# Triangle layers in one kernel: the variance of each chunk as four 32-column products, roots taken on 128 partitions and moved by small DMAs

## What is computed

```python
xn = layernorm(x, norm_g, norm_b)            # (x - mu) * rsqrt(var + eps) * g + b
left = xn @ Wl.T * m * sigmoid(xn @ Wlg.T)   # m: mask, layers 0 and 1 only
right = xn @ Wr.T * m * sigmoid(xn @ Wrg.T)
out_gate = sigmoid(xn @ Wog.T)
out = einsum('bikd,bjkd->bijd', left, right) # in layer 3: bimc,bmjc->bijc
out = layernorm(out, ...) * out_gate
return out @ Wout.T
```

## Time and profile before

| | |
|---|---|
| median of three runs | 2096.42 us |
| the profiled execution: its own time | 2098.47 us |
| its span | 2096.6 us |
| mean granted clock of TensorE | 0.958 of full speed |
| TensorE busy | 1779.0 us, 85% |
| ScalarE busy | 1372.8 us, 65% |
| VectorE busy | 1326.5 us, 63% |
| GpSimd busy | 1006.1 us, 48% |
| transfers | 496 MB, 237 GB/s in the mean |

### The profile page before, as it was taken

One profiled execution on the slowest core, in us unless ns is written; L12 is line 12 of the kernel. 1 busy time (PEld: TensorE's weight loads), 2 busy tenths in 40 slices (PEclk: granted clock), 3 DMA queues, 4 the chain that ended last, 5 costly groups with the idle time before them and its releaser, 6 DMA issues. The chain is left out here.

```text
span 2096.6 us, 40996 instructions
## 1 busy us (share of the span) xinstructions
PE 1779.0 (85%) x10389; PEld 1041.3 (50%) x10389; DVE 1326.5 (63%) x2984; ACT 1372.8 (65%) x2541; POOL 1006.1 (48%) x916
## 2 busy tenths in 40 slices
PE   0899997797998899995599799789799999699776
PEld 0445454685554445453255477633344444588433
DVE  7566666124763677776977388466377778344675
ACT  0577876355996788874499666477577787344554
POOL 0267678003991577776699300089222223000599
PEclk9999999798999999998899899999899999899999
DMA  7357876774996355546399666089547777845599
GB/s 325 123 181 235 246 231 218 268 290 170 366 367 232 101 188 173 187 149 253 135 349 366 242 217 209 32 316 375 193 150 232 234 236 216 296 179 222 187 397 377
DMA packets 326949, 496.17 MB, mean 237 GB/s; under 512 B 22828, under 2 KB 188463, under 8 KB 320439
## 3 DMA queue, kind: packets, MB, share of 16 engines
q1 hardware_dynamic: 326838, 494.93, 68.4%
HBM read 285.12 MB, written 197.13 MB: 230 GB/s over the span
## 5 line engine op out<-in xcount | busy, mean ns | idle before, releaser
L804 POOL TENSOR_TENSOR lo<-xn,hi 128x512 f16<-128x512 f32 x192 | 224.0, 1167 | 374.1 <-DVE hi L736 230.6
L601 PE MATMUL ps<-w_heads,hi 64*128 64x256 f16 x3072 | 294.0, 274 | 10.2 <-DVE sig L750 4.5
L1112 ACT ACTIVATE O<-ps 128x512 f32 (+1 forms) x144 | 151.8, 1054 | 190.5 <-PE ps L1033 190.5
L750 DVE SCALAR_TENSOR_TENSOR sig<-ps,largest,sig 128x512 f32<-128x512 f32 x256 | 180.8, 746 | 142.8 <-ACT sig L664 141.9
L664 ACT ACTIVATE sig<-ps,largest 128x512 f32<-128x512 f32 x384 | 246.2, 692 | 30.7 <-PE ps L601 28.6
L645 ACT ACTIVATE zs<-ps,shift 128x512 f32<-128x512 f32 x192 | 131.9, 687 | 191.4 <-PE ps L569 188.5
L1349 POOL TENSOR_TENSOR shared<-O,out_rs 128x128 f32<-128x128 f32 (+1 forms) x112 | 76.4, 684 | 370.8 <-DVE out_rs L1249 369.8
L601 PEld LDWEIGHTS ps<-w_heads,hi 64*128 64x128 f16 x3072 | 153.9, 95 | 167.1 <-DVE sig L750 67.3
L1397 PEld LDWEIGHTS ps<-ident,shared 128*128 128x128 f32 (+1 forms) x1024 | 120.0, 133 | 225.5 <-issue 96.4
L1397 PE MATMUL ps<-ident,shared 128*128 128x128 f32 (+1 forms) x1024 | 160.8, 282 | 75.6 <-POOL shared L1349 48.9
L601 PE MATMUL ps<-w_heads,lo 64*128 64x256 f16 x1536 | 213.5, 273 | 0.0
(11 more groups left out here) (164 smaller groups left out, 3724.3 us busy)
## 6 DMA issues: line engine op xcount, KB each, us to landing
shared<-left_right SPq DMA_DIRECT2D x34, 2048.0 KB, 12.0
shared<-gate SPq DMA_DIRECT2D x224, 256.0 KB, 4.6
gate<-gates SPq DMA_DIRECT2D x96, 512.0 KB, 2.9
x_dram<-shared SPq DMA_DIRECT2D x192, 256.0 KB, 4.3
shared<-x_dram SPq DMA_DIRECT2D x192, 256.0 KB, 4.7
xs<-x_dram SPq DMA_DIRECT2D x64, 512.0 KB, 4.2
left_right<-stage SPq DMA_DIRECT2D x64, 448.0 KB, 6.0
left_right<-shared SPq DMA_DIRECT2D x64, 448.0 KB, 5.7
```

The lines of the kernel that those rows point to most:

```text
L601: last = pe.matmul(PAIR[row][:, g, kb * S:kb * S + S], tokens[half, q % 8, at:at + P], k["w_heads"][half, part, :], start=(step == 0), sto ...
L750: dve.scalar_tensor_tensor(dst, pair(row, 1), k["largest"][:, 1:2], factor, ALU.mult, ALU.mult).then_inc(pair_read.sem, 1)
L804: pool.tensor_tensor(lo[:, q % 8, :], xn[:, q % 2, :], hi[:, q % 8, :], ALU.subtract).then_inc(c["lo_done"].sem, 1)
L1112: act.activation(o_of(ch), ps[h % 4 // 2][:, h % 2, :].rearrange("p (b g i) -> p b g i", b=2, g=2), ACT.Copy).then_inc(c["o_copied"].sem, 1)
```

## The change

The weights of `variance` have 32 columns instead of 128, and each chunk's product is made as four, one for each quarter of 128 tokens, into partitions 0, 32, 64 and 96 of the bank. The bank then holds 128 x 128 numbers, of which 16 rows in each 32 are the variances of a batch. Ln and Exp, and the split into three terms, work on 128 x 128. The terms go into a new tile, terms, and twelve DMAs from SP (three terms times four quarters, each 16 partitions of 256 bytes) move them into r_terms, where the spread reads them as before. A spread waits for the twelve moves of its batch. The split is cut in two halves, five and four steps ahead; the moves are issued three steps ahead. `variance` stands before the heads on TensorE, `root` before the sigmoids on ScalarE. CENTER is 14 and VARIANCE 13, so that 14 chunks are centered before the loop; x is loaded 18 ahead, into the same eight slots. hi and lo have four slots and not eight. SP's loop over the bodies is written out.

```diff
+QUAD = 32
...
-            "basis": sb("basis", [P, P]), "var_w": sb("var_w", [P, 2 * BATCH - 2 + P]), "ident": sb("ident", [P, P]),
+            "basis": sb("basis", [P, P]), "var_w": sb("var_w", [P, 2 * BATCH - 2 + QUAD]), "ident": sb("ident", [P, P]),
...
-                        ("xc_in", 4), ("gc_in", 4), ("x_out", 4)):
+                        ("xc_in", 4), ("gc_in", 4), ("x_out", 4), ("r_moved", 2)):
...
-    LOAD, CENTER, VARIANCE, SPLIT, NORM = 14, 12, 11, 3, 2
+    LOAD, CENTER, VARIANCE, SPLIT, MOVE, NORM = 18, 14, 13, (5, 4), 3, 2
+    R_PARTS, MOVES = 3, 3 * CH // P
...
-        log_var, r, r_rest, r_mid = (sb(name, [2 * BATCH, CH], dt) for name, dt in
-                                     (("log_var", F32), ("r", F32), ("r_rest", F32), ("r_mid", BF16)))
+        log_var, r, r_rest = sb("log_var", [P, P]), sb("r", [P, P]), sb("r_rest", [P, P])
+        terms = sb("terms", [P, 3, P], BF16)
         r_terms = sb("r_terms", [P, 2, CH], BF16)
-        xn, hi, lo = sb("xn", [P, 2, CH]), sb("hi", [P, 8, CH], F16), sb("lo", [P, 8, CH], F16)
+        xn, hi, lo = sb("xn", [P, 2, CH]), sb("hi", [P, 4, CH], F16), sb("lo", [P, 4, CH], F16)
...
-        Z, VAR, R, GATE = ps[0][:, 0, :], ps[0][:, 1, :], ps[1][:, 0, :], ps[1][:, 1, :]
+        Z, VAR, R, GATE = ps[0][:, 0, :], ps[0][:, 1, 0:P], ps[1][:, 0, :], ps[1][:, 1, :]
...
+            def move_r(i, b):
+
+                batch = i * (BODY // BATCH) + b
+                moved = c[f"r_moved{b % 2}"]
+                sp.wait_ge(c["r_split"].sem, c["r_split"](batch + 1))
+                sp.wait_ge(c["spread_done"].sem, c["spread_done"](batch * BATCH - BATCH))
+                for term in range(3):
+                    for quad in range(CH // P):
+                        sp.dma_start(r_terms[R_PART * term:R_PART * term + 2 * BATCH, b % 2, quad * P:quad * P + P],
+                                     terms[quad * QUAD:quad * QUAD + 2 * BATCH, term, :]).then_inc(moved.sem, 16)
+
             def step(i, q, more, first=False):
+                if more(MOVE) and (q + MOVE) % BATCH == 0:
+                    move_r(i, (q + MOVE) // BATCH)
...
             for q in range(2, LOAD, 2):
                 load(0, q)
+            move_r(0, 0)
             for q in range(BODY):
                 step(0, q, lambda lead: True, first=True)
-            with sp.Fori(1, bodies - 1) as i:
+            for i in range(1, bodies):
                 for q in range(BODY):
-                    step(i, q, lambda lead: True)
-            for q in range(BODY):
-                step(bodies - 1, q, lambda lead: q + lead < BODY)
+                    step(i, q, lambda lead: i * BODY + q + lead < NCH)
...
+                at = q % BATCH
                 pe.wait_ge(c["sq_done"].sem, c["sq_done"](m + 1))
-                at = q % BATCH
                 if at == 0:
-                    batch = i * (BODY // BATCH) + q // BATCH
-                    pe.wait_ge(c["log_done"].sem, c["log_done"](batch))
-                w = k["var_w"][:, 2 * (BATCH - 1 - at):2 * (BATCH - 1 - at) + P]
-                pe.matmul(VAR, w, sq[:, q % 2, :], start=(at == 0), stop=(at == BATCH - 1)).then_inc(c["var_done"].sem, 1)
+                    pe.wait_ge(c["log_done"].sem, c["log_done"](i * (BODY // BATCH) + q // BATCH))
+                first = 2 * (BATCH - 1 - at)
+                for quad in range(CH // P):
+                    last = pe.matmul(VAR[quad * QUAD:quad * QUAD + QUAD, :], k["var_w"][:, first:first + QUAD],
+                                     sq[:, q % 2, quad * P:quad * P + P], start=(at == 0), stop=(at == BATCH - 1))
+                last.then_inc(c["var_done"].sem, 1)
...
-                pe.wait_ge(c["r_split"].sem, c["r_split"](i * (BODY // BATCH) + b + 1))
+                moved = c[f"r_moved{b % 2}"]
+                pe.wait_ge(moved.sem, moved((i * (BODY // BATCH // 2) + b // 2 + 1) * MOVES * 16))
...
             def step(i, q, more):
                 if more(NORM):
                     spread(i, q + NORM)
                 if more(CENTER):
                     center(i, q + CENTER, Z, i * BODY + q + CENTER)
+                if more(VARIANCE):
+                    variance(i, q + VARIANCE)
                 heads(i, q, 0)
                 heads(i, q, 1)
                 out_gate(i, q)
-                if more(VARIANCE):
-                    variance(i, q + VARIANCE)
...
-                act.activation(log_var[:], VAR[0:2 * BATCH, :], ACT.Ln, bias=k["unit"][0:2 * BATCH, 2:3]).then_inc(c["log_done"].sem, 1)
+                act.activation(log_var[:], VAR, ACT.Ln, bias=k["unit"][:, 2:3]).then_inc(c["log_done"].sem, 1)
...
+            def step(i, q, more):
+                m = i * BODY + q
+                if more(CENTER):
+                    square(i, q + CENTER, Z)
                 if more(VARIANCE) and (q + VARIANCE) % BATCH == BATCH - 1:
                     root(i, (q + VARIANCE) // BATCH)
-
-            def step(i, q, more):
-                m = i * BODY + q
-                if more(CENTER):
-                    square(i, q + CENTER, Z)
                 gate_pair(i, q, 0)
                 gate_pair(i, q, 1)
-                root_step(i, q, more)
...
+                moved = c[f"r_moved{(b - 1) % 2}"]
+                dve.wait_ge(moved.sem, moved((i * (BODY // BATCH // 2) + (b - 1) // 2 + 1) * MOVES * 16))
-
-                dve.wait_ge(c["spread_done"].sem, c["spread_done"](batch * BATCH - BATCH))
+                dve.tensor_copy(terms[:, 0, :], r[:]).then_inc(parts.sem, 1)
+                dve.wait_ge(parts.sem, parts(batch * R_PARTS + 1))
+                dve.tensor_tensor(r_rest[:], r[:], terms[:, 0, :], ALU.subtract).then_inc(parts.sem, 1)
+
+            def split_low(i, b):
+
+                batch = i * (BODY // BATCH) + b
+                dve.wait_ge(parts.sem, parts(batch * R_PARTS + 2))
+                dve.tensor_copy(terms[:, 1, :], r_rest[:]).then_inc(parts.sem, 1)
+                dve.wait_ge(parts.sem, parts(batch * R_PARTS + 3))
+                dve.tensor_tensor(terms[:, 2, :], r_rest[:], terms[:, 1, :], ALU.subtract).then_inc(c["r_split"].sem, 1)
...
-                    dve.wait_ge(c["gate_mm_done"].sem, c["gate_mm_done"](m - 7))
-                    dve.tensor_tensor(hi[:, q % 8, :], zs[:, q % 16, :], R, ALU.mult).then_inc(c["hi_done"].sem, 1)
+                    dve.wait_ge(c["gate_mm_done"].sem, c["gate_mm_done"](m - 3))
...
-                if more(SPLIT) and (q + SPLIT) % BATCH == 0:
-                    split_r(i, (q + SPLIT) // BATCH)
+                for split, lead in zip((split_high, split_low), SPLIT):
+                    if more(lead) and (q + lead) % BATCH == 0:
+                        split(i, (q + lead) // BATCH)
                 left_and_right(i, q)
...
-            split_r(0, 0)
+            split_high(0, 0)
+            split_low(0, 0)
```

## The result

The changed kernel takes 2225.01 us (median of 4 runs, 2223.74 to 2227.33), the kernel before on the same chip 2095.92 us: a ratio of 1.063, 95% interval 1.062 to 1.065. It was forecast at 2105 us with a range up to 2142. The sign was right, the size was not, and the result lies outside the range.

The account below looks back on a forecast made before the run. TensorE was taken as the bound, at 4.10 us per ordinary chunk. Terms summed to +1.4, +4.7 and +3.3 us in layers 0, 1 and 3, together +9, giving 2105 us, range 2062 to 2142.

Parts of the forecast that it names:

- case A: The forecaster's own case, with the spread waiting for the moves: 2105 us, own range 2090 to 2122, chance 0.42.
- (d): Twelve SP moves: 6.1 us from terms to spread, stalls of +23, +21, +20.3 us in layers 0, 1, 3.
- h: Start of a chunk's heads on TensorE, zero point for root and stall times; terms whole at h+11.6, layer 3 h+12.8.
- (c): Split on VectorE: five operations on 16x512 become four on 128x128, about 0.23 to 0.29 us each; nothing gained.
- Rival D: The stalls let TensorE's clock fall: 14 stalls of about 3 us add up to 24 us, 2129 us; chance 0.10.
- (a): Variance product on TensorE: four quarter products overlap partly, 0.55 us, ordinary chunk 3.79 us; -15.5 us per layer.
- fourfold overlap: All four variance quarters at once on TensorE: chunk 3.46 us, -19, 2086 us; chance 0.28 together with rival C.
- rival C: Faster: moves all but hidden at each batch's first spread, about 4.0 us not 6.1: 2061 us; chance with fourfold overlap 0.28.
- (b): Root on ScalarE: 3.94 becomes 3.3 us, placed ahead of sigmoids; -3.5, -0.7, -1.4 us in layers 0, 1, 3.
- (e): Start of a layer: the first spread now waits for the moves, +2.9 us per layer.
- (f): x loaded four chunks ahead of centering, not two, removes layer 0's one wait for x, 2.46 us; halved rings cost nothing.

Follow-up runs that it names:

- Experiments 2 and 5: 2: only the first term's four moves, 2061.20 us; 5: terms through DRAM, four issues and not twelve, 2092.18 us; both against the kernel after.
- Run 4: Kernel after, with 24 products that nothing reads keeping TensorE busy while it waits for the moves: 2185.37 us, ratio 1.045.
- run 10: Root put back behind the sigmoids, on the kernel with terms through DRAM and earlier split and moves: 2040.90 us, ratio 0.975.
- runs 7 and 11: 7: kernel after with the whole chain further ahead, 2109.28 us; 11: that lead, terms through DRAM, root behind the sigmoids, 2036.88 us.

## Why the prediction was wrong

The mechanism was the one of case A: the spread of each batch's first chunk waits for the moves. The place and the cause were right; the price was not, and two things it takes with it were missed.

**(d), the step that failed.** It priced a move's issue by the smallest issue of the trace, 0.29 us, and 0.34 with the gap; the runs show 0.63. Twelve take 7.53 and not 4.1 us, and terms to spread 8.7 and not 6.1; even the upper bound, 8.4, was below that. The row taken, a load of two rows from DRAM, was near in bytes but not in kind. The trace before had 24 issues in layer 0 with both ends in SBUF, in the very group whose landings the prediction used:

```profile
L441 SPq DMA_DIRECT2D shared<-stage x12: 616/621/742, 127.4 to 273.8; - x12
L441 SPq DMA_DIRECT2D shared<-shared x12: 636/638/680, 165.8 to 308.6; - x12
```

Twelve at 0.62 are 7.4 us. The landing, 2.0 behind the twelve issues, was too high: the last one lands 1.7 us after its issue begins, 1.1 after it ends. Experiments 2 and 5 show that the count of issues is the lever.

**When the terms are whole.** The sum had h + 11.6. With h at 226.64 they are whole at 240.11, so h + 13.5. Each half of the split takes 1.7 us (0.57 and 1.12; in layer 1 2.3, in layer 3 1.4) where (c) had about 0.5 from a cast of 0.226, which is right where GpSimd is idle (0.23 and 0.29 at 80.44), and the two chunks behind the root take 4.16 and not 3.79. TensorE wanted the spread at h + 16.4 (243.07), not 15.2. The landing at h + 22.2, less 16.4, is the stall of 5.8 us; the sum had 3.3. Over all the waits are 130 us and not 64 for the stalls and 18 at the starts of layers: 48 of the missing 120 us.

**Rival D was not a rival but a companion.** It was set against A with 0.10 and priced at 24 us on 14 stalls. The argument against it, roots that idle TensorE 2 us at a clock of 1.00, doesn't carry: the stretches cited the earlier trace rows have TensorE busy throughout, the roots of the kernel before idle it 1.65 to 1.73 us, and the clock fell behind 17 of the kernel after's own 21 roots, where it idles 2.2 to 2.8 us. Behind each of the 24 stalls 3.4 us are granted 0.50 to 0.55. Run 4 measures 40 us for 21 of them. It belonged as a term in every case with long stalls; that would have moved the range's upper end too.

**(a)** had the right sign and too small a size: 0.55 was forecast for the four products, 0.36 was measured, with the switch to the heads in it. The argument that order is kept, so that first and second pass of a quarter block the next quarter, is wrong: the single records in the trace show the four first passes starting within 25 ns, then the four second passes. Chunks are 3.60 us, so this term gave -25 and not -15.5 per layer. The fourfold overlap that stood beside rival C had it, with 3.46. The switch was misread as well: the 0.96 at a 32-wide product was taken for no drain and the same 0.96 for 0.10 of a switch; the kernel after has 0.95 there (258.91 to 259.86).

**(b)** the root's own time was right, 3.31 against 3.3. What it costs TensorE was not: in the mean of six roots 3.7, 4.7 and 4.4 us in layers 0, 1 and 3 of the kernel without moves (at one root of layer 0, 5.88 + 4.16 + 4.15 less 3 x 3.60 = 3.4; where the clock falls 3.9 to 4.1), not 1.9, 1.9 and 2.6. With chunks of 3.60 ScalarE's 2.97 leaves 0.63 us per chunk to pay the debt, and the place ahead of the sigmoids puts it on TensorE's path; run 10 shows 1.7 for the other place. Seven roots in each of three layers: 90 us and not 45.

**Together.** Waits +48, clock +40, roots +45 and chunks -28 are 105 of the 120 us. Some 7 more lie at the starts of the layers: outside the stretches from a layer's first gate product to its last, the kernel after takes 21.6 us more than the kernel without moves, of which 14.4 are the three waits for the moves; each is followed by a granted clock of 0.50 to 0.52, and run 4 did not fill them. Without moves the sum had -73 (9.4 less 64.3 and 18.3), so 2023 us; the run took 2045.8, and roots and chunks explain 17 of these 23. What is left, some 8 us, was not traced to a cause.

**(e) and (f)** were small terms. At the centering the kernel after has no wait for x of the size of the earlier trace rows, as forecast; runs 7 and 11 show how little room there is.

## What to carry to other kernels

Count the issues, not the bytes: the row of small DMAs on one queue cost its number times the issue time before the last could land, and all that is queued behind it (here the loads of x) pays too. Price an issue by one whose two ends are in the same memories, if the trace has it. Here that was the difference between 0.29 and 0.62 us; the runs changed ends and shape together, so they don't show which of the two sets the time. And when a change shortens the bound engine's step, ask which of the other engines still has room for its burst. Here the root is ScalarE's burst, and its place in the order decides what it costs TensorE: in layer 1 4.1 us ahead of the sigmoids, 1.7 behind them.

## What the runs showed that I had not expected

- An issue on SP from SBUF to SBUF (16 rows of 256 bytes) takes 0.59 us by its record and 0.63 to the next; from SBUF to DRAM (96 KB) 0.33, from DRAM back to SBUF 0.43 (medians). The way through DRAM, two landings in a row, took 4.1 us with 4 issues against 8.7 with 12.
- Four f32 products with 32 weight columns in the four quarters of the array run at once, both passes: the four first passes start within 0.02 us of each other, and it is 0.36 us to the next product against 0.99 in one quarter.
- After 5.8 us without work TensorE is granted 0.50 for the next 3.4 us and 0.68 for the 4 after that. From the spread to the gate product behind such a wait it takes 2.6 us longer. After waits of 2.2 to 2.8 us at a root the clock fell in some cases (17 of 21 in the kernel after) and not in others, after 1.65 to 1.73 in none.
- In layer 0, beside GpSimd's products, a 128x128 cast on VectorE takes 0.57 us and a 128x128 subtraction 1.12, where the two take 0.23 and 0.29 with GpSimd idle; in layer 1 they take 1.18 and 1.15, in layer 3 0.22 and 1.21. So a quarter of the columns did not give a quarter of the time. No run changed GpSimd's work alone.
